# Reordering the three-term products, the state product and GpSimd's queue in a fused linear-attention and FP4 feed-forward kernel

## The reference

```
x = x + attn(layernorm(x)) @ Wo + bo          # linear attention, 16 heads of 64
    q, k = relu(xn Wq) + 0.001, relu(xn Wk) + 0.001 ; v = xn Wv
    attn = (q · cumsum(k vᵀ)) / (q · cumsum(k))      # causal
x = x + ffn(layernorm(x))                      # 256 -> 704 -> 256
    fp4(t): per block of 16, scale = max|t| / 6, values rounded to the FP4 grid
    h = silu(fp4(x) fp4(Wg)ᵀ) * (fp4(x) fp4(Wu)ᵀ) ; out = fp4(h) fp4(Wd)ᵀ
```

## Time and profile before

| | |
|---|---|
| median of 3 runs | 1792.27 us (1790.91, 1792.27, 1792.31) |
| profiled execution, its own time | 1787.68 us |
| its span | 1786.0 us, 46951 instructions |
| PE busy | 1692.8 us (95%), 20388 matmuls |
| PEld busy | 1591.0 us (89%) |
| DVE, ACT, POOL busy | 1138.6 us (64%), 657.2 us (37%), 434.3 us (24%) |
| chain that ended last, by engine | PE 73%; DVE 14%; POOL 7%; ACT 3%; issue 2% |

### The profile page before, as it was taken

One profiled execution on the slowest core, in us unless ns is written; L12 is line 12 of the kernel. 1 busy time (PEld: TensorE's weight loads), 2 busy tenths in 40 slices (PEclk: granted clock), 3 DMA queues, 4 the chain that ended last, 5 costly groups with the idle time before them and its releaser, 6 DMA issues.

```text
span 1786.0 us, 46951 instructions
## 1 busy us (share of the span) xinstructions
PE 1692.8 (95%) x20388; PEld 1591.0 (89%) x20388; DVE 1138.6 (64%) x2458; ACT 657.2 (37%) x1233; POOL 434.3 (24%) x643
## 2 busy tenths in 40 slices
PE   5689999999999999999999999999999999999985
PEld 4589999999999999999999999999999999999985
DVE  6856666666666756666766666756666665666664
ACT  4143333333333333333334343334333333333322
POOL 5522122222212222212222212222212222221211
PEclk8899999999999999999999999999999999999998
DMA  3000000000000000000000000000000000000000
GB/s 136 28 2 13 13 10 14 13 5 13 14 10 14 14 4 13 14 11 13 14 13 5 13 10 14 13 13 5 14 13 11 14 13 5 14 14 10 8 8 9
DMA packets 21962, 26.26 MB, mean 15 GB/s; under 512 B 1792, under 2 KB 20736, under 8 KB 21760
## 3 DMA queue, kind: packets, MB, share of 16 engines
q1 hardware_dynamic: 21760, 23.27, 4.1%
HBM read 14.88 MB, written 8.39 MB: 13 GB/s over the span
## 4 chain that ended last, share of the span: by engine, by line
PE 73%; DVE 14%; POOL 7%; ACT 3%; issue 2%; DMA 0%; POOLq 0%; DVEq 0%
PE bank L378 51%; PE bank L452 5%; PE bank L425 5%; POOL qkT L780 4%; PE bank L491 3%; PE bank L435 3%; DVE probs L970 3%; POOL hq L757 2%; DVE h_scaled L884 2%; DVE h_scaled L882 2%; PE bank L481 2%; PE bank L468 2%; DVE attn L1004 1%; PE bank L521 1%; ACT h_square L714 1%
## 5 line engine op out<-in xcount | busy, mean ns | idle before, releaser
L378 PE MATMUL bank<-xT_hi,wqk_hi 128*128 128x256 f32 x1024 | 295.1, 288 | 0.0
L378 PE MATMUL bank<-xT_lo,wqk_hi 128*128 128x256 f32 x1024 | 286.6, 280 | 0.0
L378 PE MATMUL bank<-xT_hi,wqk_lo 128*128 128x256 f32 x1024 | 286.0, 279 | 0.0
L613 ACT ACTIVATE qkT<-bank 128x512 f32<-128x512 f32 x256 | 153.2, 598 | 212.3 <-PE bank L378 212.3
L378 PEld LDWEIGHTS bank<-xT_lo,wqk_hi 128*128 128x128 f32 x1024 | 193.2, 189 | 0.0
L378 PEld LDWEIGHTS bank<-xT_hi,wqk_lo 128*128 128x128 f32 x1024 | 192.9, 188 | 0.0
L378 PEld LDWEIGHTS bank<-xT_hi,wqk_hi 128*128 128x128 f32 x1024 | 192.8, 188 | 0.0
L780 POOL TENSOR_SCALAR qkT<-qkT 128x512 f32<-128x512 f32 x256 | 154.9, 619 | 151.8 <-ACT qkT L613 151.8
L841 DVE TENSOR_TENSOR hqT_lo<-bank,hqT_hi 128x512 fp32r<-128x512 f32 (+1 forms) x128 | 68.3, 556 | 175.5 <-ACT hqT_hi L666 175.5
L970 DVE TENSOR_TENSOR probs<-bank,causal 128x512 f32<-128x512 f32 x256 | 164.4, 683 | 14.6 <-PE bank L425 14.1
L425 PE MATMUL bank<-qkT 64*128 64x128 f32 x2048 | 141.9, 284 | 18.0 <-POOL qkT L780 14.9
(11 more groups left out here) (141 smaller groups left out, 4157.0 us busy)
## 6 DMA issues: line engine op xcount, KB each, us to landing
x_in<-in_L_attn_x SPq DMA_DIRECT2D x32, 256.0 KB, 2.8
out<-out_sb SPq DMA_DIRECT2D x64, 128.0 KB, 1.7
probs<-in_L_attn_Wv SPq DMA_DIRECT2D x1, 1024.0 KB, 5.0
qkT<-in_L_attn_Wq SPq DMA_DIRECT2D x1, 1024.0 KB, 7.1
qkT<-in_L_attn_Wk SPq DMA_DIRECT2D x1, 1024.0 KB, 9.2
attn<-in_L_attn_Wo SPq DMA_DIRECT2D x1, 512.0 KB, 10.1
k_tok<-in_L_attn_Wo SPq DMA_DIRECT2D x1, 512.0 KB, 11.1
hid<-in_L_ffn_w_down SPq DMA_DIRECT2D x1, 352.0 KB, 2.9
```

The lines of the kernel that those rows point to most:

```text
L378: last = pe.matmul(dst, lhs_at(lhs[i], kt), rhs_at(rhs[j], kt), start=(kt == 0 and n == 0), stop=(kt == k_tiles - 1 and n == 2))
L613: act.activation(flat(qkT[:, 2 * m:2 * m + 2, :]), bank[bank_of["qk", c, n]][:], ACT.Relu).then_inc(qk_relu, 1)
```

## The change

- Products: `product3` is replaced by `product`, which does one of the three terms for all slices; a caller issues hi·hi, then the term with the other operand's low part that needs no new activation, then the one with the activation's low part. The wait for the high part stands ahead of the first, the wait for the low part ahead of the last (`gate_up`, `down`, `project_out`, `project_v`; `project_qk` keeps its single wait). The very first `project_v` also starts on wv_hi and waits for wv_lo after its first term.
- `attend`: where c > 0, the state product of both halves comes first and opens the accumulation; probs times v follows and raises `av_done` after each half.
- `turn_xq` and the copy of its high part on ACT: in odd steps that project, after `project_qk` 0 and 1 (and their relu on ACT) instead of ahead of them. The bank list follows.
- POOL: `add_bias` after `xq`; `add_eps` 4 and 5 ahead of `rstd_1`, 6 and 7 behind it, and the second `scale_h` (it makes hq) last.

```diff
-            def product3(dst, lhs, rhs, k_tiles, lhs_at, rhs_at):
-                last = None
+            def product(dst, lhs_at, rhs_at, k_tiles, first=False, last=False):
                 for kt in range(k_tiles):
-                    for n, (i, j) in enumerate(((0, 0), (0, 1), (1, 0))):
-                        last = pe.matmul(dst, lhs_at(lhs[i], kt), rhs_at(rhs[j], kt),
-                                         start=(kt == 0 and n == 0), stop=(kt == k_tiles - 1 and n == 2))
-                return last
+                    at = pe.matmul(dst, lhs_at(kt), rhs_at(kt), start=first and kt == 0,
+                                   stop=last and kt == k_tiles - 1)
+                return at
...
             def gate_up(b, c, g, half):
-                pe.wait_ge(xqT_ready, g + 1)
+                pe.wait_ge(xqT_hi_ready, g + 1)
...
+                    product(dst, lambda kt: xqT_hi[:, kt, :], lambda kt: w_hi[:, kt, cols], KD, first=True)
+                    product(dst, lambda kt: xqT_hi[:, kt, :], lambda kt: w_lo[:, kt, cols], KD)
+                    pe.wait_ge(xqT_ready, g + 1)
+                    product(dst, lambda kt: xqT_lo[:, kt, :], lambda kt: w_hi[:, kt, cols], KD, last=True
+                            ).then_inc(done, 1)
...
             def project_v(b, c, u, t, first=0):
-                pe.wait_ge(xT_ready, u + 1)
+                pe.wait_ge(xT_hi_ready, u + 1)
...
+                    product(dst, lambda kt: xT_hi[:, kt, at], lambda kt: wv_hi[:, kt, cols], KD, first=True)
+                    if c == "first" and not t:
+                        pe.wait_ge(attn_w_ready, 1)
...
+                    if not n:
+                        pe.wait_ge(xT_ready, u + 1)
...
             def attend(b, c, g, u):
...
+                if c:
+                    for half in range(2):
...
+                                    pe.matmul(bank[to[half][odd]][th * DH:th * DH + DH, j * VW:(j + 1) * VW],
+                                              qkT[rows, pair, at:at + DH], state[rows, pair, :],
+                                              start=j == 0, stop=False, skip_group_check=True)
                 for half in range(2):
                     pe.wait_ge(probs_ready, 4 * g + 2 * half + 2)
...
-                                                 start=j == 0, stop=c == 0, skip_group_check=True)
-                    if c == 0:
-                        last.then_inc(av_done, 1)
-                if c:
...
+                                                 start=not c and j == 0, stop=True, skip_group_check=True)
+                    last.then_inc(av_done, 1)
...
             def step(b, c):                                  # PE
-                if before:
+                if before and not project:
                     turn_xq(b, c, g - 1)
...
                     if project:
                         project_qk(b, c, u + 1, 2 * n, 2 * n + 2)
+                    if project and before and n == 0:
+                        turn_xq(b, c, g - 1)
...
             def step(b, c):                                  # POOL
-                if c % 2 == 0 and exists(u + 1, ALL_HALVES):
-                    add_bias(u + 1, 1 - c // 2)
...
                     pool.tensor_tensor(blocks(xq[:], XB), blocks(x_scaled[:], XB), each(x_scale[:], XB),
                                        ALU.mult).then_inc(xq_ready, 1)
+                if c % 2 == 0 and exists(u + 1, ALL_HALVES):
+                    add_bias(u + 1, 1 - c // 2)
...
+                if project:
+                    for n in range(4, 6):
+                        add_eps(u + 1, n)
                 if c % 2 == 1 and exists(u + 2, ALL_HALVES) and exists(g, ALL_CHUNKS):
                     rstd_1(u + 2)
+                if project:
+                    for n in range(6, PAIRS):
+                        add_eps(u + 1, n)
                 if c % 2 == 1 and exists(g - 1, ALL_CHUNKS):
                     scale_h(g - 1)
-                if project:
-                    for n in range(4, PAIRS):
-                        add_eps(u + 1, n)
```

More of the change, by code:

```diff
@@ L220, in build_program @@
             keys += [("v", c, n) for n in range(2)] + [("av", c, n) for n in range(4)]
-            keys += [("kv", c, n) for n in range(2) if update] + [("xq", c, 0)]
+            keys += [("kv", c, n) for n in range(2) if update] + [("xq", c, 0)] * (not odd)
             for n in range(2):
-                keys += [("qk", c, 2 * n), ("qk", c, 2 * n + 1)] * odd + [("hq", c, n)]
+                keys += [("qk", c, 2 * n), ("qk", c, 2 * n + 1)] * odd + [("xq", c, 0)] * (odd and n == 0)
+                keys += [("hq", c, n)]
             for n in range(2):
@@ L407, in project_qk @@
                     for s in range(2):
[L408 to L411, removed]
+                        at = slice((2 * QK_ORDER[n] + s) * P, (2 * QK_ORDER[n] + s + 1) * P)
+                        dst = bank[k][:, s * HALF * P:(s + 1) * HALF * P]
+                        product(dst, lambda kt: wqk_hi[:, kt, at], lambda kt: xT_hi[:, kt, :], KD, first=True)
+                        product(dst, lambda kt: wqk_lo[:, kt, at], lambda kt: xT_hi[:, kt, :], KD)
+                        last = product(dst, lambda kt: wqk_hi[:, kt, at], lambda kt: xT_lo[:, kt, :], KD, last=True)
                     last.then_inc(qk_projected, 1)
@@ L524, in down @@
             def down(b, c, g):
+                k = banks.take(pe, ("down", c, 0), b, out_ready, lambda b: CHUNKS * b + c - 1)
+                dst = bank[k][:, 0:DIM]
+                pe.wait_ge(hqT_hi_ready, 2 * (g + 1))
+                product(dst, lambda kt: hqT_hi[:, kt, :], lambda kt: wd_hi[:, kt, :], KF, first=True)
+                product(dst, lambda kt: hqT_hi[:, kt, :], lambda kt: wd_lo[:, kt, :], KF)
                 pe.wait_ge(hqT_ready, 2 * (g + 1))
-                k = banks.take(pe, ("down", c, 0), b, out_ready, lambda b: CHUNKS * b + c - 1)
-                product3(bank[k][:, 0:DIM], (hqT_hi, hqT_lo), (wd_hi, wd_lo), KF,
-                         lambda w, kt: w[:, kt, :], lambda w, kt: w[:, kt, :]).then_inc(down_done, 1)
+                product(dst, lambda kt: hqT_lo[:, kt, :], lambda kt: wd_hi[:, kt, :], KF, last=True
+                        ).then_inc(down_done, 1)
             pe.wait_ge(constants_ready, 3)
             turn_x(0, "first", 0)
-            pe.wait_ge(attn_w_ready, 1)
+            pe.wait_ge(attn_w_hi, 1)
             for t in range(HALF):
@@ L690, in step @@
                                    ACT.Copy).then_inc(xqT_hi_ready, 1)
+                project = c % 2 == 1 and now and following
+                if before and not project:
+                    high_xq()
                 high_ffn_weights(jobs_at(g, "update"))
-                project = c % 2 == 1 and now and following
                 for n in range(2):
```

46 lines of the change are left out of this document (24 added, 22 removed).

## The result

The changed kernel takes 1738.97 us (median of 4 runs, 1735.05 to 1739.14); the kernel before took 1792.29 in the same set of runs (4 runs, 1790.91 to 1793.55). The ratio is 0.9697, 95% interval 0.9681 to 0.9714: 53.3 us less, forecast 1742. The two aren't alike: TensorE's granted clock, averaged over the execution, was 0.988 in the one of before and 0.984 in that of after. In 22 executions of the kernel before whose clock is on record, the four at 0.988 took 1787.7 to 1787.9 and the others, at 0.982 to 0.986, 1789.0 to 1792.3; of the changed kernel, the one at 0.987 took 1735.05 and the three at 0.984 took 1738.9 to 1739.1.

A forecast was written before the change was run, and what follows sets the result against it. PE was taken as the bound, with three steady waits to remove. Terms 22.7 + 14.0 + 8.5 + 2.9 + 0 + 1.5 = 49.6 us, from 1792.27, gave 1742.7, stated as 1742; range for 8 in 10: 1733 to 1765.

The forecast's parts named there:

- Two of the prediction's bounds: Forecast's span from its terms: 1736 with all upper ends, 1755 with scores' 22.7 whole and the others at lower ends.
- Scores, 22.7: Scores in chunks 0 and 2 stop waiting for POOL's adds: 0.76 and 0.56 a time, 2.9 in the first sequence.
- `gate_up`, 14.0: Even steps' gate_up starts on xq's high part without awaiting DVE's low part: 31 x 0.45 us saved.
- `turn_xq`, 8.5: Odd steps that project: PE no longer waits for POOL's xq, 16 x 0.53 us saved (8.0 to 9.4).
- What is late next: Check whether work behind moved instructions becomes late; for scale_h's hq and turn_xq's followers it claimed no new wait.
- `attend`, 2.9: State product first means one tile-shape change fewer: 0.09 in chunks 1 and 2, 32 times; bounds 0 to 2.9.
- Products, 0: Some 448 added waits within products, satisfied except in gate_up, and unchanged matmuls and weight loads: taken to cost 0.
- Ends, 1.5: First project_v and last down start before low parts are ready: 1.5 us together, 0 to 2.6.
- rival C: Within products, even satisfied waits stop matmuls overlapping: 0.16 each, 448 x 0.16 = 72 us, so 1814; 6%.
- A: Another wait, turn_xq for xq in chunks 0 and 2, takes back the scores' gain: 19.8 us lost, 1762; 17%.
- B: POOL's moved adds and DVE's rounding of h hinder each other, making x2 late: 26 us, 1768; 4%.
- D: Nothing moves: later stalls replace those removed, step length being set by a loop through DVE: 1792; 3%.

The follow-up runs named there:

- e1: Changed kernel with POOL's old order of the late adds (add_eps 4 to 7 behind the second scale_h): 1763.25 us, ratio 0.9846.
- e9: Kernel before with POOL's new order of the late adds alone: 1766.42 us against 1791.59, ratio 0.986.
- e2: Changed kernel with gate_up again waiting for the low part of xq ahead of its first matmul: 1752.18 us, ratio 0.9791.
- e3: Changed kernel with turn_xq and its ACT copy again ahead of project_qk 0 and 1 in odd steps: 1743.92 us, ratio 0.9743.
- e10: e8 plus, in step 1, DVE making the low part of the last weights ahead of xq's: 1731.52 us, ratio 0.9667.
- e4: Changed kernel with probs times v ahead of the state product again: 1744.61 us, ratio 0.9745.
- e6: Changed kernel with one more, always satisfied wait ahead of every matmul of every product: 1737.25 us, ratio 0.9704.
- e5: Changed kernel with all products written as before (three terms per k-tile, waits ahead), other parts kept: 1755.58 us, ratio 0.9804.
- e7: Changed kernel with each late add (4 to 7) done twice on POOL: 1737.97 us, ratio 0.971.
- e11: e10 plus 189 useless matmuls keeping PE busy at six points of fill and drain: 1725.12 us, ratio 0.9631.
- e8: Changed kernel with one PSUM bank left out ahead of chunk 0's scores, avoiding project_out's bank: 1735.66 us, ratio 0.9694.

## Why the prediction was right

The forecast was 1742, with 49.6 gained; measured were 1738.97 and 53.3, or 52 to 53 between executions of the same granted clock. The direction, the mechanism and the three large terms held. A small term, `attend`, was undersized, and with it the steady part: 2.93 a sequence were forecast (0.76 + 0.56 + 0.9 + 0.53 + 0.18) and 3.12 came. Two of the prediction's bounds don't follow from its own terms: all upper ends (22.7, 15.8, 9.4, 2.9, 2.6) give 53.4 and so 1739, not 1736, and all lower ends beside the scores' 22.7 (8.6, 8.0, 0, 0) give 39.3 and so 1753, not 1755; the upper end of `gate_up` is also 31 x 0.5 = 15.5, not 15.8. By the right sum the measured median lies at the very edge of what the terms allowed, not well inside.

- **Scores, 22.7.** Right. The stages lost 0.56 and 0.76 a sequence, and 4.89 became 1.99 in the first sequence's chunk 2, the 2.90 forecast. e1 and e9 price it at 24.3 and 25.2, each by itself. What was said to be next, `scale_h`, isn't late: `turn_hq` starts when the stages before it let it.
- **`gate_up`, 14.0.** Right: 0.46 for 0.45 a time, start 0.06 after the high part for 0.05; e2 gives 13.2. The estimate from starts was the good one; the idle times of the list would have said 8.6.
- **`turn_xq`, 8.5.** Right in the steady part: 0.57 less ahead of `turn_xq`, 0.49 net by e3. One consequence was overlooked. "What is late next" was asked for the steady steps alone, and found nothing; in step 1 DVE's queue holds the low part of the last weights behind xq's, and PE waits 0.4 for it by the profile (0.67 by starts: 3.56 for those 24 matmuls, 2.89 in e10). e10 takes it away.
- **`attend`, 2.9.** Undersized. The working from the earlier trace rows took state into probs as 1.10 and probs into update_state as 1.92 (measured 1.09 and 1.92), but let update_state be equally long, and it is 0.05 shorter; chunk 3 and the products behind were taken at 0 and bring a few hundredths each. e4: 0.46 a sequence for the 0.18 taken, 5.6 in the median, beyond the upper bound of 2.9.
- **Products, 0.** Right, and the sharpest result: at rival C's 0.16 per wait, the 6,850 waits that e6 adds would have cost 1,096 us; they cost nothing.
- **Ends, 1.5.** The pair of profiled executions seems to say that this failed (head 0.2 longer, tail only 1.3 shorter). The other runs say that it held, and that two other things hid it.

The head first. The first `project_v` started at 10.78 for 13.16 and its third matmul at 13.11 for 14.18, 1.07 ahead. But in both kernels matmuls start 0.43 apart at first and 0.23 apart only from about 18.4 (before) and 18.8 (after), so with fewer left to run at the fast pace the lead shrank to 0.30 at the next stage. At `project_qk` of step 1 it is 0.67 (94.33 for 95.00); the wait for the low part of `wd` and `turn_xq` within it turn that into 0.23 behind at `gate_up` (100.92 for 100.69). The start of `turn_x` in the first sequence's chunk 2 prices both edits: 113.87 and 114.18 with neither (before, e9), 113.08 with only the products of the two (e3), 115.63 with only the late `turn_xq` (e5), 113.21 to 114.16 with both (after, e1, e2, e4, e6, e7). So the products bring 1 to 2 us there and the late `turn_xq` takes 0.6 to 1.6 back; that cost was the step overlooked.

Then the drain. From the last `turn_hq` to the end it is 9.60 to 9.71 with the old products (before, e5, e9) and 8.96 to 9.01 with the new (all others but e11), so the 0.68 by which the last `down` starts earlier (2.85 before, 2.17 after) is won in each. The stretch from the last sequence's chunk 3 scores to the end was nevertheless 53.53 before and 54.74 after. What differs is the granted clock, and the edit doesn't settle it: e6 and e7 have PE's order of the changed kernel there and took 53.67 and 51.42, with 0.71 and 0.83 granted in the last 40 us, while e9, with the products of before, took 55.35 with 0.74. The last 40 us of e7:

```profile
1694.00:1734.00 40.00, 24.11 (x149) 22.99 (x147) 19.59 (x39) 8.55 (x17) 4.13 (x5) 0.83 0.03 10
```

That the clock of the ends moves the time by several us from one execution to the next was in no term of the prediction. e11, at 1.00, takes 47.68 for that stretch.

The rivals. **A** would have shown as PE waiting for xq in chunks 0 and 2; no such wait exists, and e1 and e9 show the parts adding up. **B** has its mechanism but not its effect. Groups of lines of the changed kernel (busy, mean ns | idle ahead):

```profile
L911 DVE SCALAR_TENSOR_TENSOR h_scaled<-h_square,h_scaled 128x704 f32<-128x704 bf16 x64 | 63.8, 997 | 51.7 <-ACT h_square L740 51.7
...
L1118 DVE TENSOR_TENSOR x<-bank,x_bias 128x256 f32<-128x256 f32 x64 | 27.1, 424 | 63.2 <-PE bank L377 63.2
...
L806 POOL TENSOR_SCALAR qkT<-qkT 128x512 f32<-128x512 f32 x256 | 183.8, 722 | 345.8 <-ACT qkT L634 345.8
```

and of e1, where the adds don't run beside the rounding:

```profile
L908 DVE SCALAR_TENSOR_TENSOR h_scaled<-h_square,h_scaled 128x704 f32<-128x704 bf16 x64 | 56.9, 889 | 64.6 <-ACT h_square L740 64.6
...
L806 POOL TENSOR_SCALAR qkT<-qkT 128x512 f32<-128x512 f32 x256 | 155.5, 621 | 142.1 <-ACT qkT L634 142.1
```

The rounding is 0.11 longer a time and the add 0.10, with single instructions held much longer (1.35 for 0.89). DVE's idle time ahead of x2 was 76.1 before, is 74.0 in e1 and 63.2 now: 13 us were eaten from 76, 11 of them by the new place of the adds. These rows agree in kind with the exclusion that the Trainium skill states in "SBUF — State Buffer", section "Who interferes with whom". **C** fell with e6. **D** fell with the result.

What stays open: why the drain and the fill are granted more of the clock in some executions than in others, what makes up the rest of the 4.1 us between e8 and e10, and the hundredths in the products of e4. The conditions for a lower clock weren't measured, only its price.

## What to carry to other kernels

Price a wait by the starts around it against a step without the wait; the list of waits gave 0.28 where 0.46 was lost. Split a product's wait by its terms when one operand's part comes later, since satisfied waits cost nothing (e6), and put short jobs that the bound engine needs ahead of a long one on a queue with slack. For every instruction that is moved later, walk its queue in the first steps too, where other jobs are queued behind it; and in the fill and the drain, where PE waits anyway, useless matmuls ahead of the next products gave 6.4 us. Before two profiles are subtracted, compare the granted clock of their ends: here 0.988 against 0.984 in the mean went with 48.5 us where 53 were gained.

## What the hardware showed that was not expected

- Some 6,850 more weight loads that carry a satisfied wait cost 0 us (e6, 1737.25 against 1738.97; sequence 103.29 against 103.28).
- Leaving a run of 128x64 tiles for another tile shape costs PE 0.10 us: the same 64 matmuls take 2.02 when 64x64 (e4) or 128x128 tiles (chunk 3) follow, and 1.92 when 128x64 tiles follow. What the border from 64x64 into 128x64 tiles costs can't be told: both orders have it.
- The extra adds of e7 took 903 ns each beside DVE's work, where the adds of e1, in their old place, took 621, and still nothing reached PE.
- A wait for a bank can be missing from the list under its releaser: 0.19 a sequence stood under "issue" of the weight load until e8 removed it, about 2.8 us in all.
- The same drain is granted a different clock in different executions: 0.71 in the last 40 us of the changed kernel and of e6, 0.83 in e7, with the same order on PE, and 54.74, 53.67 and 51.42 us from chunk 3's last scores to the end. Useless matmuls held it at 1.00 in e11, where that stretch took 47.68; with those in the head they gave 6.4 us.
